# Condition matrices in pairs of rows, token tiles loaded even channels first, ten warming matmuls instead of fifteen

## The reference

```python
x            # (32, 64, 1024)      itok_B_0_15  # (32,), values 0..15
cond_w       # (16, 64, 64)
w1, b1       # (1024, 4096), (4096,)     w2, b2   # (4096, 1024), (1024,)

W = cond_w[itok_B_0_15]                          # one 64x64 matrix per sample
y = einsum('bct,bcd->bdt', x, W)
h = gelu(einsum('bsd,df->bsf', y, w1) + b1)      # tanh approximation
out = x + einsum('bsf,fd->bsd', h, w2) + b2
```

## Time and profile before

| what | value |
|---|---|
| median of 3 runs | 1259.47 us (1259.41 to 1259.98) |
| the profiled execution's own time | 1260.09 us |
| its span, first to last instruction | 1258.3 us |
| PE busy | 1253.7 us (100% of the span) |
| DVE, ACT, POOL busy | 832.5, 567.3, 186.2 us |
| moved by DMA | 249.28 MB, mean 198 GB/s |
| granted clock of TensorE, mean over the span | 1.000 |

### The profile page before, as it was taken

One profiled execution on the slowest core, in us unless ns is written; L12 is line 12 of the kernel. 1 busy time (PEld: TensorE's weight loads), 2 busy tenths in 40 slices (PEclk: granted clock), 3 DMA queues, 4 the chain that ended last, 5 costly groups with the idle time before them and its releaser, 6 DMA issues.

```text
span 1258.3 us, 15369 instructions
## 1 busy us (share of the span) xinstructions
PE 1253.7 (100%) x5662; PEld 1043.7 (83%) x5662; DVE 832.5 (66%) x1091; ACT 567.3 (45%) x969; POOL 186.2 (15%) x93
## 2 busy tenths in 40 slices
PE   9999999999999999999999999999999999999998
PEld 9888888888888888888888888888888888888887
DVE  5977787676577767656557455555547767784764
ACT  4744554454444444444434444444444444444442
POOL 4262223321000000000034233312200000000000
PEclk9999999999999999999999999999999999999999
DMA  9576655764997322249845324554189932323431
GB/s 345 164 269 248 246 196 221 277 251 181 388 389 278 101 88 96 101 171 358 306 147 183 104 117 170 184 184 148 75 332 394 347 136 91 101 101 100 155 130 52
DMA packets 94234, 249.28 MB, mean 198 GB/s; under 512 B 7344, under 2 KB 15824, under 8 KB 92752
## 3 DMA queue, kind: packets, MB, share of 16 engines
q1 hardware_dynamic: 93408, 248.01, 54.3%
q10 hardware_dynamic: 720, 0.28, 0.1%
q0 software_dynamic: 32, 0.00, 0.0%
HBM read 162.28 MB, written 85.98 MB: 197 GB/s over the span
## 4 chain that ended last, share of the span: by engine, by line
PE 99%; DVE 0%; DVEq 0%; issue 0%
PE ps L553 48%; PE ps L569 48%; PE ps L498 1%; PE ps L513 1%; PE ps L579 1%; DVE acc L873 0%; DVE acc L972 0%; DVEq L66 0%; DVE ones L903 0%
## 5 line engine op out<-in xcount | busy, mean ns | idle before, releaser
L553 PE MATMUL ps<-y,lhs 128*128 128x512 f32 x2688 | 611.0, 389 | 0.0
L569 PE MATMUL ps<-rhs,lhs 128*128 128x512 f32 x2688 | 609.6, 389 | 0.0
L569 PEld LDWEIGHTS ps<-rhs,lhs 128*128 128x128 f32 x2688 | 504.5, 188 | 104.8
L553 PEld LDWEIGHTS ps<-y,lhs 128*128 128x128 f32 x2688 | 504.1, 188 | 104.4
L705 ACT ACTIVATE lhs<-h_raw 128x512 fp32r<-128x512 f32 x224 | 141.6, 632 | 345.8 <-PE ps L569 340.1
L854 DVE TENSOR_TENSOR lhs<-h_raw,lhs 128x512 fp32r<-128x512 f32 x224 | 155.1, 692 | 188.4 <-ACT lhs L705 188.4
L795 DVE TENSOR_TENSOR lhs<-w_raw,lhs 128x512 fp32r<-128x512 f32 x128 | 117.5, 920 | 125.4 <-ACT lhs L633 125.2
L633 ACT ACTIVATE lhs<-w_raw 128x512 fp32r<-128x512 f32 x128 | 80.9, 633 | 169.5 <-PE ps L553 163.4
L857 DVE TENSOR_TENSOR rhs<-W,rhs 128x512 fp32r<-128x512 f32 x224 | 153.4, 685 | 0.0
L795 DVE TENSOR_TENSOR lhs<-s_w,lhs 128x512 fp32r<-128x512 f32 x96 | 91.2, 952 | 88.1 <-ACT lhs L633 88.1
L466 POOL TENSOR_TENSOR s_w<-w_raw 128x1024 f32<-128x1024 f32 x16 | 48.1, 3006 | 621.1 <-PE ps L569 354.0
(11 more groups left out here) (35 smaller groups left out, 293.2 us busy)
## 6 DMA issues: line engine op xcount, KB each, us to landing
h_raw<-h_mem SPq DMA_DIRECT2D x112, 512.0 KB, 3.3
w_raw<-in_L_ffn_inter_w_dram SPq DMA_DIRECT2D x32, 1024.0 KB, 8.7
h_mem<-hs SPq DMA_DIRECT2D x64, 512.0 KB, 4.6
W<-in_L_ffn_output_w_dram SPq DMA_DIRECT2D x32, 1024.0 KB, 12.4
h_mem<-c SPq DMA_DIRECT2D x48, 512.0 KB, 5.7
y_mem<-y_out SPq DMA_DIRECT2D x28, 512.0 KB, 3.1
y<-y_mem SPq DMA_DIRECT2D x7, 2048.0 KB, 13.0
acc<-in_x_dram SPq DMA_DIRECT2D x16, 512.0 KB, 8.5
```

Of the source, the lines that this page charges most:

```text
L553: last = nc.tensor.matmul(ps[:, bank, :], w[:, k, :], y[i][:, part, k, :], start=(i in FRESH and k == 0 and u == 0), stop=(k == KH - 1 and ...
L569: last = nc.tensor.matmul(ps[:, bank2(h, j, tb), :], lhs[s % RING][:, a, blk(tb)], rhs[r][:, w, :], start=(j in FRESH and q == 0 and u == ...
```

## The change

The rows of a condition matrix are taken in pairs. `cond_all` becomes 32 partitions (the pair `q`) by 16 sets by 128 columns (even row, then odd row), so each contiguous run is 512 bytes instead of 256; it moves from 204 KiB to 80 KiB, where later the block `y5` lies. A token tile now has the even channels of both samples in partitions 0 to 63 and the odd ones in 64 to 127; each tile is still loaded by one DMA (tile 0 by two). A pick becomes two copies of 32x64, one for the even and one for the odd rows, behind one register load. The zeros fill all of `wdiag`: the half of pass 0 on DVE, that of pass 1 on POOL. POOL keeps the pass 1 picks of tiles 2 to 7; ACT takes those of tile 0, DVE those of tile 1. PE does 10 matmuls on ones instead of 15.

```diff
-    WARM = 15
+    WARM = 10
...
+    x_con = x.rearrange("(h j s) (q r) t -> h j r (s q) t", h=PASSES, s=PER, r=2)
...
-    cond_sets = cond_w.rearrange("s c d -> c s d")
+    cond_pairs = cond_w.rearrange("s (q r) d -> q s (r d)", r=2)
...
-        cond_all = at("cond_all", 204, [SETS, C])[0:C]
+        cond_all = at("cond_all", 80, [SETS, 2 * C])[0:C // 2]
...
-            rows = slice(s * C, (s + 1) * C)
-            return wdiag[rows, j:j + 1, rows], cond_all[:, bass.ds(which, 1), :]
+            cols = slice(s * C, (s + 1) * C)
+            return [(wdiag[(PER * r + s) * C // 2:(PER * r + s + 1) * C // 2, j:j + 1, cols],
+                     cond_all[:, bass.ds(which, 1), r * C:(r + 1) * C]) for r in range(2)]
...
-            sp.dma_start(cond_all[:, 0:SETS // 2], cond_sets[:, 0:SETS // 2]).then_inc(cond_in, 16)
-            sp.dma_start(x0[:, 0, 0:BANK], x_tok[0, :, 0, 0:BANK]).then_inc(x0_half, 16)
-            sp.dma_start(x0[:, 0, BANK:D], x_tok[0, :, 0, BANK:D]).then_inc(x0_in[0], 16)
+            sp.dma_start(cond_all[:, 0:SETS // 2], cond_pairs[:, 0:SETS // 2]).then_inc(cond_in, 16)
+            sp.dma_start(x0[:, 0, 0:BANK], x_con[0, 0, :, :, 0:BANK]).then_inc(x0_half, 16)
+            sp.dma_start(x0[:, 0, BANK:D], x_con[0, 0, :, :, BANK:D]).then_inc(x0_in[0], 16)
             for j in range(1, TILES):
-                sp.dma_start(x0[:, j, :], x_tok[0, :, j, :]).then_inc(x0_in[j], 16)
+                sp.dma_start(x0[:, j, :], x_con[0, j]).then_inc(x0_in[j], 16)
             load_w1(0, 0)
             for j in range(TILES):
                 if j == TILES - 2:
                     sp.wait_ge(cond_done, 2 * KB)
-                sp.dma_start(x1[j][:], x_tok[1, :, j, :]).then_inc(x1_in[j], 16)
+                sp.dma_start(x1[j][:], x_con[1, j]).then_inc(x1_in[j], 16)
...
         def _(pool):
-            nc.gpsimd.memset(wdiag[0:C, :, C:P], 0.0).then_inc(wdiag_zero, 1)
-            nc.gpsimd.memset(wdiag[C:P, :, 0:C], 0.0).then_inc(wdiag_zero, 1)
+            nc.gpsimd.memset(wdiag[:, TILES:PASSES * TILES, :], 0.0).then_inc(wdiag1_zero, 1)
...
             for i in range(0, TILES * PER, 3):
-                to, of = pick(pool, i)
-                nc.gpsimd.tensor_copy(to, of).then_inc(picked[0], 1)
-            pool.wait_ge(picked[0], 6)
...
-            picks1(0, TILES)
+                for to, of in pick(pool, i):
+                    nc.gpsimd.tensor_copy(to, of).then_inc(picked[0], 1)
+            pool.wait_ge(picked[0], 12)
+
+            for i in range((TILES + 2) * PER, PASSES * TILES * PER):
+                for to, of in pick(pool, i):
+                    nc.gpsimd.tensor_copy(to, of).then_inc(picked1[0], 1)
+            pool.wait_ge(picked1[0], 2 * (TILES - 2) * PER)
...
             def cond1(j):
-                pe.wait_ge(picked1, PER * (j + 1))
+                if j < 2:
+                    pe.wait_ge(picked1[1 + j], 2 * PER)
+                else:
+                    pe.wait_ge(picked1[0], 2 * PER * (j - 1))
...
-            pe.wait_ge(wdiag_zero, 2)
...
             for i in range(1, TILES * PER, 3):
-                to, of = pick(act, i)
-                nc.scalar.activation(to, of, ACT.Copy).then_inc(picked[1], 1)
+                for to, of in pick(act, i):
+                    nc.scalar.activation(to, of, ACT.Copy).then_inc(picked[1], 1)
+            act.wait_ge(wdiag1_zero, 1)
+            for i in range((TILES + 0) * PER, (TILES + 1) * PER):
+                for to, of in pick(act, i):
+                    nc.scalar.activation(to, of, ACT.Copy).then_inc(picked1[1], 1)
...
+                            if c == 8:
+                                act.wait_ge(picked1[0], 2 * (TILES - 2) * PER)
                             y_high({3: 2, 5: 3, 7: 4, 8: 5, 10: 6}[c])
...
             nc.vector.memset(ones[:], 1.0).then_inc(ones_made, 1)
+            nc.vector.memset(wdiag[:, 0:TILES, :], 0.0).then_inc(wdiag_zero, 1)
...
             for i in range(2, TILES * PER, 3):
-                to, of = pick(dve, i)
-                nc.vector.tensor_copy(to, of).then_inc(picked[2], 1)
+                for to, of in pick(dve, i):
+                    nc.vector.tensor_copy(to, of).then_inc(picked[2], 1)
+            dve.wait_ge(wdiag1_zero, 1)
+            for i in range((TILES + 1) * PER, (TILES + 2) * PER):
+                for to, of in pick(dve, i):
+                    nc.vector.tensor_copy(to, of).then_inc(picked1[2], 1)
```

More of the change, by code:

```diff
@@ L131, in build @@
         ones_made = sem("ones_made")
-        wdiag_zero = sem("wdiag_zero")
+        wdiag_zero, wdiag1_zero = sem("wdiag_zero"), sem("wdiag1_zero")
         picked = [sem(f"picked_{e}") for e in ("pool", "act", "dve")]
-        picked1 = sem("picked1")
+        picked1 = [sem(f"picked1_{e}") for e in ("pool", "act", "dve")]
         s_made = [sem(f"s_made{i + 1}") for i in range(4)]
@@ L432, in _ @@
             pool.dma_start(itok_sb[0:1], itok.rearrange("(o b) -> o b", o=1)).then_inc(itok_in, 16)
-            nc.gpsimd.memset(wdiag[0:C, :, C:P], 0.0).then_inc(wdiag_zero, 1)
-            nc.gpsimd.memset(wdiag[C:P, :, 0:C], 0.0).then_inc(wdiag_zero, 1)
+            nc.gpsimd.memset(wdiag[:, TILES:PASSES * TILES, :], 0.0).then_inc(wdiag1_zero, 1)
             pool.wait_ge(itok_in, 16)
             pool.wait_ge(cond_in, 32)
+            pool.wait_ge(wdiag_zero, 1)
+            pool.wait_ge(wdiag1_zero, 1)
             for i in range(0, TILES * PER, 3):
-                to, of = pick(pool, i)
-                nc.gpsimd.tensor_copy(to, of).then_inc(picked[0], 1)
-            pool.wait_ge(picked[0], 6)
[L442 to L446, removed]
-            picks1(0, TILES)
+                for to, of in pick(pool, i):
[5 more added lines that the diff above has]
+            pool.wait_ge(picked1[0], 2 * (TILES - 2) * PER)
             for h in range(PASSES):
@@ L491, in cond @@
                     for e in range(3):
-                        pe.wait_ge(picked[e], len(range(e, PER * (j + 1), 3)))
+                        pe.wait_ge(picked[e], 2 * len(range(e, PER * (j + 1), 3)))
                     for kb in range(KB):
@@ L724, in y1_high @@
                 nc.scalar.activation(y1_out[item % 2][:, 0, :], y1_in[:, (0, 0, 0, 3, 1, 2, 2)[i], :], ACT.Copy).then_inc(y1_hi, 1)
-            act.dma_start(cond_all[:, SETS // 2:SETS], cond_sets[:, SETS // 2:SETS]).then_inc(cond_in, 16)
+            act.dma_start(cond_all[:, SETS // 2:SETS], cond_pairs[:, SETS // 2:SETS]).then_inc(cond_in, 16)
             act.dma_start(b1_rows[0:F // P], b1.rearrange("(a p) -> a p", p=P)).then_inc(b1_in, 16)
@@ L732, in _ @@
             act.wait_ge(cond_in, 32)
+            act.wait_ge(wdiag_zero, 1)
             for i in range(1, TILES * PER, 3):
-                to, of = pick(act, i)
-                nc.scalar.activation(to, of, ACT.Copy).then_inc(picked[1], 1)
+                for to, of in pick(act, i):
[4 more added lines that the diff above has]
+                    nc.scalar.activation(to, of, ACT.Copy).then_inc(picked1[1], 1)
             y_keep(0)
@@ L903, in _ @@
             nc.vector.memset(ones[:], 1.0).then_inc(ones_made, 1)
+            nc.vector.memset(wdiag[:, 0:TILES, :], 0.0).then_inc(wdiag_zero, 1)
             dve.wait_ge(itok_in, 16)
             dve.wait_ge(cond_in, 32)
+            dve.wait_ge(wdiag_zero, 1)
             for i in range(2, TILES * PER, 3):
-                to, of = pick(dve, i)
-                nc.vector.tensor_copy(to, of).then_inc(picked[2], 1)
+                for to, of in pick(dve, i):
[4 more added lines that the diff above has]
+                    nc.vector.tensor_copy(to, of).then_inc(picked1[2], 1)
             dve.wait_ge(b1_in, 16)
```

## The result

The changed kernel takes 1392.41 us (median of 6 runs, 1391.45 to 1393.38) against 1259.56 (6 runs) for the kernel before: a ratio of 1.1054, 95% interval 1.104 to 1.1069. It is 133 us slower. The profiled execution took 1392.15 us and has a span of 1390.3.

What follows compares the result with a forecast made beforehand. PE bounds the kernel from 1.21 us to the last stage. Token tiles on two engines and held stores move the mark from 63.5 to 199 us: 1260.1 + 135.5 = 1395.6, less 0.6, is 1395 us; range 1345 to 1425.

Steps and rivals of the forecast that it cites:

- The likeliest case: Token tiles on two engines, with pass 1's stores held behind them on SP's queue: 1395 us, chance 0.75.
- Two engines: Token-tile loads, counting two outermost in the source, run on two DMA engines, always the same two, moving 50.1 GB/s.
- the rival with changing pairs: Each token-tile load gets two engines, but another pair each time; PE starts 1 us later: 1260.5 us, chance 0.03.
- A tile per 10.5 us: Token-tile loads: 524,288 bytes on two engines at 401/16 GB/s each take 10.5 us instead of 1.3.
- Tile 7 of pass 0 at 87 us, the weights at 92: Start: eight tiles of pass 0 from near 3 us, then the first weights, 5.2 us, behind them in the queue.
- The hold of the stores: Stores of pass 1's product tile 0 wait behind token tiles on one queue, land near 178 us; tile 4 waits.
- the rival without hold: Two engines, but stores pass the token tiles; PE done with tile 7 near 178 us: +114.5, 1374 us, chance 0.09.
- 18 us of PE work behind the hold and 2 us for the low clock: PE's tiles 4 to 7 and steps 6 to 9, first 16 matmuls at 1.2 GHz: to 199 us.
- Nothing behind the mark: After PE finishes pass 1's last tile (63.52 us before, 199 forecast), nothing is late; 1195 us of PE follow.
- Picks, zeros, runs of the conditions at nothing: Start: two-copy picks, zeros on DVE and POOL, and 512-byte condition runs add nothing to the end time.
- the lower bound of 0.23: Picks on ACT and POOL: the second copy adds between 0.23 us (copy alone) and 0.7 us (whole pick).
- The rival of sixteen engines, 1258.6 us: All sixteen carry the tiles; first weights landing at 19.66 us cap the gain at 0.9 us; chance 0.13.

Runs made afterwards that it cites:

- 2: Kernel before, each token tile loaded from two blocks of 64 contiguous rows, 8 samples apart (outermost count 2, no gaps): 1393.17 us.
- 3: Kernel before, each token tile loaded from every second of 256 rows, 128 counted outermost: 1260.31 us.
- 4: Kernel before, each token tile loaded from four blocks of 32 contiguous rows (outermost count 4): 1315.78 us.
- 5: Kernel before, each token tile loaded from eight blocks of 16 rows (outermost count 8): 1274.89 us.
- 6: Changed kernel, stores of pass 1's product issued by ACT on its own queue behind its copies, instead of by SP: 1382.9 us.
- 7: Changed kernel, SP issues the stores of tiles 0 and 1 of pass 1's product ahead of token tiles 6 and 7 of pass 1: 1388.22 us.
- 9: Kernel before with ten matmuls on ones instead of fifteen, nothing else: 1260.15 us against 1259.82, ratio 1.0002.
- 8: Changed kernel with the token tiles' rows loaded in the old order, 128 rows outermost: 1259.49 us against 1259.82, ratio 1.0000.
- 1: Changed kernel, each token tile loaded by two DMAs of 64 rows, 64 counted outermost: 1267.43 us against 1260.01, ratio 1.0063.
- 11: Experiment 1 with pass 0's upper halves issued by ACT on its queue, biases moved to SP behind the weights: 1278.43 us, ratio 1.0148.
- 12: Kernel before, each token tile loaded by two DMAs of 64 contiguous rows, same data: 1267.62 us against 1259.91, ratio 1.0063.
- 10: Kernel before with ten ones, first half of the first weights issued ahead of token tile 7: 1260.00 us against 1259.85, ratio 1.0002.

## Why the prediction was right

It said 1395 us with 1345 to 1425; measured are 1392.4. The likeliest case came true, and the steps can be checked one by one.

- **Two engines** (the step that decided): right, and shown three ways. Count two alone in the old kernel brings the whole loss (2), gaps alone none (3), and the share of engines goes with the count, 0.13, 0.26, 0.50 (2, 4, 5). The rule cited from the Trainium skill agrees with all counts run here (2, 4, 8, 64, 128 in the source); that the engines are the lowest-numbered ones no view shows. That they are the same for each load is shown by the rate: the rival with changing pairs would have kept it, and it fell.
- **A tile per 10.5 us** from 401/16 GB/s: 9.98 measured. An engine moves 26.5 GB/s when two run and 26 when four do, some 5% more than its share in a full set. The term was 5% too large, 8 us over 16 tiles.
- **Tile 7 of pass 0 at 87 us, the weights at 92**: 87.1 and 89.7. That the first fits to 0.1 us is luck: the pace is faster (4 us less over eight tiles), but the tiles start to flow 2 us later (tile 0 is there at 14.9 us, tile 5 at 64.8), and tiles 6 and 7 lose 2.4 us beside the weights. The weights come only 2.6 us behind tile 7, not 5.2: the prediction took all of them at the rate of sixteen engines, while the two slow ones had to carry only their two sixteenths of the first half (131 KB, 2.5 us at 52 GB/s, an estimate).
- **The hold of the stores**: right as a place, 173.5 us instead of 178, and the 32.3 us that PE waited there are in the waits above. The stores landed where the prediction puts them, just behind the tiles: by 9.98 us a tile from tile 3 at 132.2, tile 7 is due at 172.1 (an estimate). What it did not have is that SP issued them only at 148.75 us: with two engines taking the packets, issuing a tile took SP 9.7 us (16.7 at most), so SP was itself stuck behind its own loads. The size of the hold was not isolated: experiments 6 and 7 took away 9.5 and 4 us of it, each putting something else in its place, so the price of 21 us for the rival without hold stays untested.
- **18 us of PE work behind the hold and 2 us for the low clock**: 20.3 us (174.8 to 195.1), of which the first 32 records took 5.79 us instead of 3.57. In one place the prediction's clock is not what the profile grants: it has the ones at 1.2 GHz, where the granted clock reads 1.00 from 2 to 8 us; what the rows show is their pace, 0.43 us instead of 0.22.
- **Nothing behind the mark**: 0.5 us there, which ten ones alone show as well (9). The mark came at 195 instead of 199; that is the 3 us by which the forecast was high. It is what is left of two errors that partly cancel: 8 us too many for the tiles, 4 us too few for their later start and for what tiles 6 and 7 lost beside the weights.
- **Picks, zeros, runs of the conditions at nothing**: right (8). A second copy adds 0.1 us to a pick (0.75 and 0.79 us a pair on ACT and POOL, against 0.65 and 0.7), less than the lower bound of 0.23.
- **The rival of sixteen engines, 1258.6 us**: its cap by the first weights holds with ten ones alone (9), but not for the rest of the change (8), whose weights land at 18.33 us instead of at 19.66 "whatever PE does". Its gain of 0.9 us is not shown: 1259.49 for the rest alone is within noise of no change. To call this case no difference was right.

## What to carry to other kernels

Reordering rows in a load leaves its bytes and its data packets as they are, and can still cost a factor of seven in rate (401 to 54 GB/s): what counted in these runs is how many pieces the outermost level of the source has (the destination had 128 in all but experiments 1, 11 and 12). Read the DMA share beside the rate: a low rate at a share of 0.13 is two engines of sixteen; a low rate at a share of 1 is something else (experiments 1 and 12 are that case). Before a load is made slower, look at what stands behind it on its queue: here PE waited 32 us for stores of 256 KB.

## What the runs showed that I had not expected

**Half the partitions, 0.6 of the rate.** Loads in two transfers of 64 partitions moved 243 and 256 GB/s with the engines' share above 1, against 401 for 128 partitions (1, 12). The Trainium skill, "SBUF — State Buffer", section "Door 1: The DMA port swizzle", has a reason: bit 6 of the partition chooses between the two ports of a cluster, so a transfer to either half reaches 8 of 16 ports. It says further, under "Can I just issue two DMAs to hit both halves?", that two transfers cannot be fused to reach all. The traces agree in direction; by the first rule alone the rate would be half, 200 GB/s (an estimate from the 401 measured), and it was 243 to 256.

**The queue holds its issuer.** With two engines in use, SP needed 9.6 us to issue a load that took it 0.44 us before (the medians of L324 here and of L320 in the kernel before). A time counted from the end of the issue then leaves out the part of a transfer's wait that has moved into the issue.

```profile
L324 SPq DMA_DIRECT2D x<-in_x_dram x7: 3944/9607/16723, 2.5 to 44.9; - x7
```

**What is issued behind a load can slow it.** With eight engines, tiles issued long before the weights slowed from 2.5 to as much as 3.9 us each once the weights were issued (5), and in the changed kernel tiles 6 and 7 of pass 0 took 11.0 and 11.3 us instead of 9.98. To put a transfer earlier also costs the one behind it: half of the first weights, issued ahead of token tile 7, landed 2.6 us earlier (17.1 instead of 19.7), and tile 7 landed only at 19.9 us (10).
